# Two-layer attention and expert kernel on one core: the second layer's k by k scores are placed in another order

## What is computed

```python
s = jnp.einsum('bihd,bjhd->bhij', k, k) * scale        # k by k scores
s = jnp.where(strict, s, -jnp.inf)                      # only earlier keys
p = softmax(s)                                          # by rows, an empty row stays 0
A = p * beta + eye(T)                                   # lower triangular, 256 x 256 per head
u = solve_triangular(A, v, lower=True)                  # forward substitution
sc = jnp.einsum('bihd,bjhd->bhij', q, k) * scale        # q by k scores
o = softmax(causal(sc)) @ u
return o @ Wo
```

## Time and profile before

| | us |
|---|---|
| median of 3 runs | 820.59 |
| lowest and highest run | 819.68 and 837.18 |
| time of the profiled execution | 820.95 |
| its span, first to last instruction | 819.1 |
| second layer's attention ahead of the first substitution, 312 to 430 | 118 |
| the four substitutions, 430 to 642 | 212 |

### The profile page before, as it was taken

One profiled execution on the slowest core, in us unless ns is written; L12 is line 12 of the kernel. 1 busy time (PEld: TensorE's weight loads), 2 busy tenths in 40 slices (PEclk: granted clock), 3 DMA queues, 4 the chain that ended last, 5 costly groups with the idle time before them and its releaser, 6 DMA issues. The chain is left out here.

```text
span 819.1 us, 17908 instructions
## 1 busy us (share of the span) xinstructions
PE 515.0 (63%) x7444; PEld 424.2 (52%) x7444; DVE 555.0 (68%) x1066; ACT 300.3 (37%) x716; POOL 227.1 (28%) x320
## 2 busy tenths in 40 slices
PE   0362555875859554327565676678886750899980
PEld 0352444764648443325443455466655540899980
DVE  6899699797969847766656684663664165667834
ACT  3354333543456340062654204523213150365520
POOL 3000000000000000104848807816830036043254
PEclk9875775986888786755586666687979555899996
DMA  8445041050000100760070150020001162666224
GB/s 307 149 76 116 1 89 28 1 117 1 2 0 2 52 0 17 159 136 5 3 155 6 40 90 7 7 47 7 10 10 12 55 245 85 245 204 235 78 58 136
DMA packets 52067, 61.30 MB, mean 75 GB/s; under 512 B 25409, under 2 KB 45393, under 8 KB 47505
## 3 DMA queue, kind: packets, MB, share of 16 engines
q1 hardware_dynamic: 50176, 55.15, 25.1%
q0 software_dynamic: 1808, 4.99, 2.0%
HBM read 45.24 MB, written 13.63 MB: 72 GB/s over the span
## 5 line engine op out<-in xcount | busy, mean ns | idle before, releaser
L888 PE MATMUL psum<-arena 32*32 32x16 f32 (+18 forms) x5608 | 357.6, 274 | 214.3 <-DVE arena L1557 75.7
L888 PEld LDWEIGHTS psum<-arena 32*32 32x32 f32 (+6 forms) x5608 | 284.4, 128 | 287.1 <-DVE arena L1557 78.4
L1994 POOL TENSOR_TENSOR arena<-arena 128x31 f32<-128x31 f32 (+15 forms) x124 | 68.4, 552 | 9.7
L1992 POOL TENSOR_TENSOR arena<-arena 128x31 f32<-128x31 f32 (+15 forms) x124 | 64.4, 519 | 9.7
L1350 ACT ACTIVATE psum<-psum,arena 128x256 f32<-128x256 f32 (+7 forms) x128 | 45.7, 364 | 30.4 <-DVE arena L1618 30.2
L1527 DVE TENSOR_TENSOR_SCAN arena<-arena 128x255 f32<-128x255 f32 x64 | 42.5, 726 | 11.4 <-ACT arena L1262 11.4
L1628 DVE TENSOR_REDUCE arena<-psum 128x2 f32<-128x512 f32 (+1 forms) x48 | 41.3, 861 | 12.5 <-PE psum L888 11.8
L1972 POOL DMA_DIRECT2D arena<-wq x1 | 0.9, 862 | 171.9 <-PE psum L888 171.9
L1319 ACT ACTIVATE arena<-psum 128x512 f32<-128x512 f32 (+1 forms) x48 | 35.4, 736 | 35.8 <-PE psum L888 35.5
L2005 POOL TENSOR_TENSOR fc_second_parts<-arena,fc_first_parts 128x2048 fp32r<-128x2048 f32 x6 | 27.9, 4650 | 63.7 <-ACT fc_first_parts L1438 63.7
L1262 ACT ACTIVATE arena<-arena 128x255 f32<-128x255 f32 x64 | 27.2, 498 | 46.6 <-DVE arena L1513 46.6
(11 more groups left out here) (179 smaller groups left out, 928.0 us busy)
## 6 DMA issues: line engine op xcount, KB each, us to landing
arena<-fc SPq DMA_DIRECT2D x16, 1024.0 KB, 5.2
arena<-parts SPq DMA_DIRECT2D x40, 256.0 KB, 4.5
parts<-arena SPq DMA_DIRECT2D x16, 384.0 KB, 3.6
arena<-parts SPq DMA_DIRECT2D x40, 128.0 KB, 5.4
dispatched<-arena SPq DMA_DIRECT2D x1, 2048.0 KB, 18.9
arena<-arena SPq DMA_DIRECT2D x128, 8.0 KB, 1.8
arena<-dispatched SPq DMA_DIRECT2D x8, 256.0 KB, 3.3
expert_rows<-arena SPq DMA_DIRECT2D x8, 256.0 KB, 2.3
```

The costliest lines, as they stand in the source:

```text
L888: return nc.tensor.matmul(out, lhsT, rhs, start=start, stop=stop)
L1992: link(G_.tensor_tensor(tmp, A3[:, k + 1:BLK, k:k + 1].to_broadcast([P, rows, w]), X3[:, k:k + 1, 0:w].to_broadcast([P, rows, w]), ALU.mult))
L1994: ins = G_.tensor_tensor(X3[:, k + 1:BLK, 0:w], X3[:, k + 1:BLK, 0:w], tmp, ALU.add)
```

## The change

Three things move, and no instruction is added or removed. In the stretch ahead of the first substitution the order of the steps is another one; the queries of batches 2 and 3 (`asked(2)`, `asked(3)`, with their `qload`) move into the first and the second substitution; and the step `inverse b` stands one piece earlier in the list. In `lag` a substitution now begins at `solve`. A wait of SyncE ahead of batch 1's `kq` loads asks for two rounded batches where it asked for four.

```diff
-    o += [("requant", 0), ("gate", 2, 0)] + keys_then_queries(0) + [("qload", 0), ("vproj", 0), ("requant", 1), ("gate", 2, 1)]
-    o += keys_then_queries(1) + [("qload", 1), ("vproj", 1), ("requant", 2), ("requant", 3), ("gate", 2, 2)]
-    o += groups("kscores", 1, 0) + [("kmax", 1, 0)] + groups("scores", 1, 0)[:4] + [("kdiag", 0), ("den", 0), ("blocks", 0)]
-    o += groups("kprobs", 1, 0) + groups("scores", 1, 0)[4:] + [("minus", 1, 0), ("max", 1, 0)]
-    o += groups("kscores", 1, 1) + [("kmax", 1, 1)] + keys_then_queries(2)
-    o += [("kdiag", 1), ("den", 1), ("blocks", 1)] + groups("kprobs", 1, 1) + groups("probs", 1, 0) + [("qload", 2), ("vproj", 2)]
+    def keys(b):
+        return [("proj", 1, b, 1), ("split", 1, b, 1)]
+
+    def asked(b):
+        return [("proj", 1, b, 0), ("split", 1, b, 0)]
+
+    ks, sc, pr = ([groups(kind, 1, b) for b in range(B)] for kind in ("kscores", "scores", "probs"))
+    o += [("requant", 0), ("gate", 2, 0)] + keys(0) + [("proj", 1, 0, 0), ("vproj", 0), ("split", 1, 0, 0), ("qload", 0)]
+    o += [ks[0][0], ("requant", 1), ks[0][1], ("gate", 2, 1)] + ks[0][2:4] + [("proj", 1, 1, 1), ks[0][4], ("kmax", 1, 0), ("split", 1, 1, 1)]
+    o += sc[0][:4] + [("kdiag", 0), ("den", 0), ("blocks", 0)] + groups("kprobs", 1, 0) + [("vproj", 1), ("requant", 2), ("requant", 3)]
+    o += [ks[1][0], sc[0][4], ks[1][1], sc[0][5], ("gate", 2, 2), ks[1][2], sc[0][6], ks[1][3], sc[0][7], ks[1][4], ("kmax", 1, 1)]
+    o += [("minus", 1, 0), ("max", 1, 0)] + asked(1) + [("qload", 1), ("kdiag", 1), ("den", 1), ("blocks", 1)]
+    o += groups("kprobs", 1, 1) + pr[0][:4] + keys(2) + pr[0][4:] + [("vproj", 2)]
...
-    ahead = [k2 + [[("gate", 2, 3)], [("proj", 1, 3, 1), ("split", 1, 3, 1)]] + d2 + [[("proj", 1, 3, 0), ("split", 1, 3, 0)], [("vproj", 3)]]
-             + queries(1),
-             k3 + [[("otr", 1, 0)]] + d3 + p1[:3] + [[("oT", 1, 0)]] + p1[3:6] + out(0)[1:] + p1[6:] + [[("qload", 3)]] + queries(2),
-             [[("otr", 1, 1)]] + p2[:3] + [[("oT", 1, 1)]] + p2[3:6] + out(1)[1:] + p2[6:] + queries(3),
+    ahead = [k2 + [[("gate", 2, 3)], keys(3)] + d2 + [asked(2), [("qload", 2), ("vproj", 3)]] + queries(1) + [[("inverse", 1)]],
+             k3 + [[("otr", 1, 0)]] + d3 + p1[:3] + [[("oT", 1, 0)]] + p1[3:6] + out(0)[1:] + p1[6:] + [asked(3), [("qload", 3)]]
+             + queries(2) + [[("inverse", 2)]],
+             [[("otr", 1, 1)]] + p2[:3] + [[("oT", 1, 1)]] + p2[3:6] + out(1)[1:] + p2[6:] + queries(3) + [[("inverse", 3)]],
...
+    o += [("inverse", 0)]
     for b in range(B):
 
-        solve = [[("inverse", b), ("solve", b, 0, 0), ("solve", b, 0, 1)]]
+        solve = [[("solve", b, 0, 0), ("solve", b, 0, 1)]]
...
-        if step[0] == "inverse":
+        if step[0] == "solve":
             solving = True
...
                             if b == 1:
-                                sp.wait_ge(x_ready, 2 * B)
+                                sp.wait_ge(x_ready, B + 2)
```

## The result

The changed kernel takes 847.82 us (median of 4 runs, 846.44 to 849.37), the kernel before 820.17 in the 4 runs beside it: a ratio of 1.034, 95% interval 1.0312 to 1.0367. It is slower by more than 2%, 3.8 us above the forecast of 844 and inside the range. The profiled execution took 846.44 us, its span 844.6, against 820.95 and 819.1.

A forecast was written before the change was run, and what follows sets the result against it. No engine is busy over 68% of the span, so chains between engines bound it. To 820.95 it added 12.3 (stretch to first fetch), 9.0 (batch 2's keys), -1.8 and 4.0 (substitutions), together 23.5: 844 us, range 826 to 855.

The forecast's parts named there:

- the prediction's first part: An earlier GpSimd start gives nothing by itself; what counts is when the steps ahead of the first fetch are through.
- Steps 1 to 3: Batch 0's scores to GpSimd's start: first maximum at 340.7, last bias at 363.1, GpSimd at about 374.5, 3.5 us earlier.
- step 1: Ahead of batch 0's first scores: VectorE idles 10 us; first maximum at 340.7 and not 354.12.
- step 2: Batch 0's groups, first maximum to last bias: four steps among them make it 22.4 us, before 12.3.
- Step 4: After `kprobs`: `vproj 1` 3.2 us, copies 0.95, two roundings beside GpSimd 5.2; batch 1's first maximum at 385.3.
- Step 5: Batch 1's scores on one ring slot: 7.1 us a turn, 30.3 us in all, costing 9.6 us.
- Step 6: From the end of batch 1's scores to the first fetch: about 25 us, fetch at 440.4, 12.3 us later.
- Rivals A and C: A: the moved steps pay as meant, about 814, chance 0.08. C: losses and gains cancel, 826, chance 0.14.
- Batch 2's keys: Right behind the first solve, TensorE waits 9.0 us for their late stack; bounds 4 and 10.
- rival B: Loads are faster where fewer things are queued, two stack waits shrink by 4.8 us each: 834; chance 0.08.
- The substitutions: First -1.8 us (bounds -3 and 0), second +4 (bounds 0 and 8), third and fourth 0.
- The fetch: Moving the fetch of the inverse earlier in the list costs and gains nothing; no VectorE instruction stood between.

The follow-up runs named there:

- experiment 5: Kernel before with only the queries of batches 2 and 3 moved into the first and second substitution, batch 2's keys staying: 823.1 us, ratio 1.0055.
- experiment 9: Changed kernel with batch 1's groups in a row, batch 0's idle time filled, batch 2's keys early and both query steps back: 826.3 us, ratio 1.0056.
- experiment 3: Changed kernel with batch 3's queries back in the first substitution, their loads staying in place: 848.0 us, ratio 1.0348.
- experiment 4: Kernel before with only the step `inverse` moved earlier in the list and `lag` changed to match: 821.2 us, ratio 1.0007.
- experiment 7: Changed kernel with batch 1's groups in a row and the four steps among batch 0's groups moved into the idle time ahead of them: 832.6 us.
- experiment 6: The kernel of experiment 5 with one SyncE wait added, so batch 2's key loads start only after `vproj 2`: 827.6 us, ratio 1.0075.

## Why the prediction was right, and where a size was off

**The account.** The medians of four kernels make a staircase down from the changed kernel: one slot for batch 1's scores 7.3 us (847.8 to 840.6), the idle time ahead of batch 0's scores with the steps among its groups 8.0 (to 832.6), the late stack 1.7 (to 830.9), the moved queries 4.6 (to 826.3). What is left, 5.8 us against 820.5, is the new order of the scores itself: its stretch ahead of the first fetch takes 117.6 us and not 111.8. There batch 1's scores are through 9.0 us sooner behind batch 0's gate than before (393.8 - 316.4 against 402.8 - 316.4), and what stands behind them takes 40.1 us and not 25.3: batch 0's last q by k groups and batch 1's queries have come behind them. The ratios give the same order of sizes with other numbers, 5.3, 10.9, 0.6 and 6.5 us and 4.6 left, so a single step is known to some 3 us, and the 1.7 can't be told from nothing. Starting batch 0's scores and GpSimd earlier returned nothing, as the prediction's first part said; in the changed kernel GpSimd's result lay ready for 24 us.

**Steps 1 to 3** held. The idle time was 9.6 us against 10, the first maximum came at 338.0 against 340.7 and GpSimd's start at 371.7 against 374.5; both are early by about the 2.0 us that the start of this execution was early, and by 0.7 and 0.8 more, which puts them just outside the windows that I had named, 340 to 342 and 372 to 377. That step 1's 10 us are a loss was tested by filling them, in one edit with taking the four steps of step 2 out from among the groups; the two weren't tried apart.

**Step 4** had one size wrong inside. `vproj 1` took from 372.23 to the copies at 379.42, 7.2 us where the prediction had 3.2 and a copy; 3.85 of them are the stop without a releaser, a term that the sum didn't have. The two roundings beside GpSimd took from 379.78 to 385.34, 5.6 us against 5.2: the first instruction 0.49 and the last 0.95. For this the prediction had weighed a rule of the Trainium skill, "SBUF — State Buffer", that the shared port is an exclusive lock; by it the estimate was 9.3 us. The trace is far nearer to the ratio taken from the earlier trace rows.

**Step 5**, one ring slot, held: the phase took 414.0 - 385.3 = 28.7 us against 30.3, a turn 6.8 to 7.0 against 7.1. Undone, it gave 7.3 us back, against 9.6 in the prediction; most of the difference is the phase, which fell from 28.7 to 16.4 us and not from 30.3 to 16.1.

**Step 6** held as a sum: 24.9 us from the last group to the fetch against about 25. Rivals A and C expected the queries' leaving to give something in the stretch. In the order before it gives nothing (experiment 5), and the trace has the stop in `vproj 2` in its place; with the loads late and that stop gone it gives 4.9 us (111.8 to 106.9), and 5.7 in the order of experiment 9. In the changed kernel itself it was not tried.

That the whole stretch came out at +12.9 against +12.3 is in part luck: counted from batch 0's gate, steps 1 to 3 were 0.8 us shorter than predicted, step 4 2.9 longer, step 5 1.6 shorter and step 6 0.1 longer.

**Batch 2's keys** held: TensorE waited 7.8 us against 9.0, bounds 4 and 10. The split's end to the last load's landing was expected at 14.0 and came to 449.23 - 435.57 = 13.7. The loads landed 3.4 to 6.8 us after their issue, and rival B fell with that. "DMA: Bandwidth & Descriptors" of the Trainium skill would have given each load some 2.3 us by the estimate in rival B; the page states that anatomy for transfers set up by GpSimd, and these are issued by SyncE.

**The substitutions** hold the term that was mis-sized: "The second gets batch 3's queries ... Together +4 (bounds 0 and 8)" measured +7.5, and the queries by themselves 9.4 (experiment 3). I had summed the durations of the instructions and taken 3 us back for an update that now covers a wait, and I had left out the wait for the solution's move, 2.1 us. The 3 us didn't come: the wait ahead of `kdiag 3` was 3.15 us before and 1.76 in the changed kernel, but 1.97 with the queries back in the first substitution as well. These 3.5 us too much, 0.6 in the first stretch and 0.5 behind the third fetch, less 2.0 of an early start and 0.5 in the first substitution, make the difference between 23.5 and 25.5; the rest up to 847.8 is the profiled execution lying 1.4 us below its median. For the first substitution, 7.8 us of wait and 70.0 - 63.3 = 6.7 us in all leave -1.1 for the gate, against -1.8. **The fetch** was nothing, as the prediction derived from the listing and experiment 4 measured.

## What to carry over

When two kinds of steps alternate on a ring of two buffers, each kind gets a single buffer, and the whole turn between its two engines is exposed; count turns and not busy time before interleaving. An early start is worth what waits at its end: look first whether the result is fetched at once. A step moved into a chain of short pieces can cost all of its work on both engines there and a wait beside it (6.7 and 9.4 us here for 4.5 us on VectorE and 2.3 to 3.9 on TensorE), and a step taken out of a stretch gives back only what doesn't reappear as a wait or a stop further on, so follow each engine to the end of the stretch and not to the first wait.

## What the hardware showed that was not expected

TensorE stops for up to 5.2 us with no releaser at fixed places of the program, and how long goes with what the DMA engines have been given just before. In `vproj 2` it was 4.79 us behind eight loads that filled the DMA engines to 104.9% of their time, with one packet of instructions moved in the stop, and nothing when those loads were issued behind it. In `vproj 1`, behind batch 1's key loads, it was 3.85 us in the changed kernel, 3.01, 2.85 and 5.22 in three kernels with the same code there (from 368 to 378 the loads held the DMA engines for 78 to 84% of the time), and 0.56 with 0.94 in experiment 7, where no load moved in that window.

That TensorE's own instructions are loaded through the same DMA engines and queue behind the data is what fits these rows, and the 13 us without a packet of the instruction queue in experiment 5; the profile doesn't say whose instructions a packet holds. Full DMA engines alone don't make the stop: in the kernel before they were just as full from 415 to 424 (101.1%) with the loads of batch 2's keys and a store, a packet of instructions came through in the us from 423, and `vproj 2` behind it ran without one. The dependence on the loads was tried once, in experiment 6; experiment 7 moved more than the loads.
